# Channel mix of a two-layer graph network: each time half times one 96x96 block, in place of two 96x192 products summed in PSUM

## The chip, the core and the metric

The kernel runs on one core of a Trainium2 chip. The metric is the device time of one execution in microseconds (us); the time of a kernel is the median of its runs. Each profile shows one execution.

## What is computed

The reference is a stack of two graph convolutions, each followed by a token feed-forward part (a mixture of experts after the first, a quantised two-layer net after the second). `x` has 16 batch items, 512 nodes, 16 channels and 12 times. Each graph convolution begins with an attention over channels, whose result then multiplies the data:

```python
def _attention(x, W1, W2, requires_value):
    sh = x.shape
    xf = x.reshape(sh[0], sh[1], -1)
    dk = xf.shape[-1]
    left = xf @ W1 @ W2
    att = jnp.einsum('bnd,bmd->bnm', left, xf) / jnp.sqrt(jnp.float32(dk))
    att = jax.nn.softmax(att, axis=-1)
    return (att @ xf).reshape(sh) if requires_value else att
...
xc = jnp.swapaxes(_attention(jnp.swapaxes(x, 1, 2), W1_c, W2_c, True), 1, 2)
xt = jnp.swapaxes(_attention(jnp.swapaxes(xc, 1, 3), W1_t, W2_t, True), 1, 3)
```

The channel mix is the product `att @ xf` of the line that makes `xc`. For each batch item a 16x16 matrix mixes the channels of every node and every time; times are not mixed with each other.

## The kernel before, in words

The program is a sequence of blocks, each ended by all engines together: normalise (n0), channel attention scores (c0), channel mix (m0), time attention scores (t0), graph convolution (g0), then normalise again, routing, experts and their sum, and the second layer with c1, m1, t1, g1, and the feed-forward part at the end. The letters are the tags in the tile names (`m_ps` is the PSUM tile of m0 and m1).

`mix_channels` (L661) is the block that the change touches; it runs twice, as m0 and as m1. The normalised data of one item lie in DRAM as 192 rows (time-major: row = time x 16 + channel) by 512 nodes. They are loaded as two halves of 96 rows: `xnT[z][0:96, h, :]` has times 0 to 5 for h = 0 and times 6 to 11 for h = 1. Four such buffers rotate (`z`).

- **SyncE** (L672) issues the loads of items 0 to 3 (L677), then two loads for later stages (`late_loads`, L183: `wt`, L186, and `adj`, L187, 1 MB each), then for each following item a load (L682) when TensorE is done with the item four before it (`mixed`).
- **VectorE** (L686) makes the moving operand: `big_matrix(b)` spreads the mixing matrix of item b (`rct`, 96 rows by 16 channels) over 192 columns (channel x 12 + time), zero where row and column have different times (`tmask`), in two operations (L693), one for each half of the rows. Two buffers (`big`, shown as `L_k`) rotate, so item b waits for `mixed` of item b - 2. In m1 it also does work of the `Ternary` class between the blocks: sums of magnitudes of the last feed-forward weights (L1830, three chunks after each of the blocks 2 to 6, the last after 7), their scale (L1840 to L1847) after block 9, and the rounding (L1853 to L1860, two chunks after each block from 10 on, four more at the end).
- **TensorE** (L721) takes for item b, for each of four node groups of 128, the two halves as stationary operands (96x128) and the two blocks as moving operands (96x192), and sums the two products in PSUM (L730). A product of f32 operands shows in the trace as two weight loads and two matmuls. The PSUM tile has two buffers. In m1 a product that sums the magnitudes across partitions (`across`) stands between items 7 and 8.
- **ScalarE** (L745) copies an item's 128x768 result to `shared` (L751). The next block (t0 or t1) begins with projections from `shared` (L590).

Outside the block three other products matter for reading costs: the residual product of the graph convolution (L900), which takes the same `xnT` halves with 97 rows against 96 columns; the logits of the second normalise (L421), 96 stationary columns against 8 moving ones; and products of the identity with itself (`keep_awake`, L287). The routing's product L1253 writes its 128 columns in runs of 8 that stand 16 apart.

Of the kernel before, what the change touches and what calls it, by code (L numbers as in the profile page):

```python
# [21 lines left out]
ALU = mybir.AluOpType  # L22
# [3 lines left out]
B, N, C, T = 16, 512, 16, 12  # L26
CT = C * T
# [6 lines left out]
P = 128  # L34
NK = N // P
HALF = CT // 2
TH = T // 2
# [24 lines left out]
def ready(n):  # L62

    return n + 1 + LEAD


def free(n, depth):

    return n + 1 + LEAD - depth


def dma_ready(i):

    return (i + 2) * 16
# [108 lines left out]
def late_loads(eng, s, d, L, late):  # L183

    p = lambda n: d[f"L{L}_conv_{n}"]
    eng.dma_start(s.wt[:, :, :, :], p("wt").rearrange("(k p) (x r) -> p k x r", p=P, r=PROJ)).then_inc(late, 16)  # L186
    eng.dma_start(s.adj[:, :, :], p("A").rearrange("(k p) m -> p k m", p=P)).then_inc(late, 16)  # L187
# [473 lines left out]
def mix_channels(nc, s, tag, xn_rows, d, L, ternary=None):  # L661

    with ExitStack() as ctx:
        (xn_in, big_done, mixed, out_done, late) = s.sems(
            tag,
            "xn_in*4 big_done mixed out_done late")
        xnT, big = [s.xnT0, s.xnT1, s.raw0, s.raw1], [s.k0, s.k1]
        psm = [ctx.enter_context(nc.psum_tensor(f"{tag}_ps{q}", [P, 2, 512], F32)) for q in range(2)]
        psq = ctx.enter_context(nc.psum_tensor(f"{tag}_psq", [P, 512], F32)) if ternary else None
        with nc.Block() as block:  # L670
            @block.sync
            def _(sp):  # L672
                for z in range(4):
                    sp.sem_inc(xn_in[z], 16)

                for z in range(4):
                    sp.dma_start(xnT[z][0:HALF, :, :], xn_rows[z]).then_inc(xn_in[z], 16)  # L677
                late_loads(sp, s, d, L, late)
                with sp.Fori(1, B // 4) as i:
                    for z in range(4):  # L680
                        sp.wait_ge(mixed, free(i * 4 + z, 4))
                        sp.dma_start(xnT[z][0:HALF, :, :], xn_rows[i * 4 + z]).then_inc(xn_in[z], 16)  # L682
                sp.wait_ge(late, 32)

            @block.vector
            def _(dve):  # L686
                dve.sem_inc(big_done, LEAD)

                def big_matrix(b):
                    if b >= 2:  # L690
                        dve.wait_ge(mixed, ready(b - 2))
                    for h in range(2):
                        last = nc.vector.tensor_tensor(  # L693
                            big[b % 2][0:HALF, h, :].rearrange("p (c t) -> p c t", t=T),
                            s.rct[0:HALF, b * C:b * C + C].unsqueeze(2).to_broadcast([HALF, C, T]),
                            s.tmask[:, h, 1, :].unsqueeze(1).to_broadcast([HALF, C, T]), ALU.mult)
                    last.then_inc(big_done, 1)

                if ternary:
                    big_matrix(0)  # L700
                    big_matrix(1)
                    ternary.begin(dve)
                    for b in range(2, HB):
                        big_matrix(b)
                        for c in range(3 * b - 6, min(3 * b - 3, 16)):
                            last = ternary.magnitude(c)
                    ternary.step(last)
                    big_matrix(HB)
                    big_matrix(HB + 1)
                    ternary.scales(dve, psq)  # L710
                    for b in range(HB + 2, B):
                        big_matrix(b)
                        ternary.round(range(2 * (b - HB - 2), 2 * (b - HB - 2) + 2))
                    for c in range(12, 16, 2):
                        ternary.round(range(c, c + 2))
                else:
                    for b in range(B):
                        big_matrix(b)

            @block.tensor  # L720
            def _(pe):  # L721
                pe.sem_inc(mixed, LEAD)

                def mix(b, z, i):
                    pe.wait_ge(xn_in[z], dma_ready(i))
                    pe.wait_ge(big_done, ready(b))
                    pe.wait_ge(out_done, free(b, 2))
                    for k in range(NK):
                        for h in range(2):
                            last = nc.tensor.matmul(psm[z % 2][:, k // 2, CT * (k % 2):CT * (k % 2) + CT],  # L730
                                                    xnT[z][0:HALF, h, P * k:P * k + P], big[z % 2][0:HALF, h, :],
                                                    start=(h == 0), stop=(h == 1))
                    last.then_inc(mixed, 1)

                with pe.Fori(0, B // 8) as i:
                    for z in range(4):
                        mix(i * 4 + z, z, i)
                if ternary:
                    ternary.across(pe, psq)
                with pe.Fori(B // 8, B // 4) as i:  # L740
                    for z in range(4):
                        mix(i * 4 + z, z, i)

            @block.scalar
            def _(act):  # L745
                act.sem_inc(out_done, LEAD)
                with act.Fori(0, B // 4) as i:
                    for z in range(4):
                        b = i * 4 + z
                        act.wait_ge(mixed, ready(b))  # L750
                        nc.scalar.activation(  # L751
                            s.shared[:, bass.ds(b * (NK * CT), NK * CT)].rearrange("p (a x) -> p a x", a=2),
                            psm[z % 2][:, :, 0:2 * CT], ACT.Copy).then_inc(out_done, 1)
# [1743 lines left out]
```

## Time and profile before

| | us |
|---|---|
| median of 3 runs | 1767.14 (1765.31 to 1768.95) |
| span of the profiled execution | 1757.2 |
| TensorE matmuls busy in it | 1443.9 (82%) |
| VectorE busy | 1063.8 (61%) |
| ScalarE busy | 769.8 (44%) |
| m0, first product to start of last eviction | 80.5 to 125.0 |
| m1, first product to end of VectorE's work | 1133.4 to 1183.1 |

Times in the trace are counted from the start of the span. PE is TensorE's matmul side, PEld its weight loads, DVE VectorE, ACT ScalarE, POOL GpSimd, SP SyncE; a q behind an engine's name is its instruction queue. Matmuls are pipelined, so the duration of one is longer than the distance to the next; a run of n that follow each other is read from start to start. The granted clock of TensorE is given in shares of 2.4 GHz: 1.00 is 2.4 GHz and 0.50 is 1.2 GHz.

### The profile page before, as it was taken

Reading aid. Unit: us, or ns where it says so; the run is one execution under the profiler, and the core shown is the slowest. Engines: PE = TensorE matmul, PEld = TensorE weight load, DVE = VectorE, ACT = ScalarE, POOL = GpSimd, SP = SyncE. Lnnn points to the kernel's source line nnn. Section 1 sums busy time; section 2 is a strip of 40 time slices with the busy share of each in tenths; the row PEclk is TensorE's granted clock in tenths of the full one; section 3 lists DMA queues with packets and bytes.
Section 4 is the critical chain, followed back from the end, with each engine's and each line's share of the span. In section 5 each row is a group of like instructions: output and inputs, shape, how many; then the busy total and the mean of one; then the engine's idle time right before and its main releaser. Section 6 shows DMA issues by size and latency. Waiting matters only on the chain. (4 is left out here: it accounts for less than half of the span.)

```text
span 1757.2 us, 27360 instructions
## 1 busy us (share of the span) xinstructions
PE 1443.9 (82%) x8574; PEld 1199.9 (68%) x8574; DVE 1063.8 (61%) x2272; ACT 769.8 (44%) x1222; POOL 610.7 (35%) x910
## 2 busy tenths in 40 slices
PE   5798999995683499999999956688999997377776
PEld 5696888885683378888888846586888886244443
DVE  5314788886446554454454326372788887478885
ACT  5323555553341132333333225222555554278885
POOL 1100465656111346655555431000356556100000
PEclk9799999998785699999999975698999999599998
DMA  7441122221662136656555368741121211112321
GB/s 244 144 122 46 48 70 72 63 81 45 200 205 92 46 97 138 128 87 131 119 111 121 46 126 298 249 110 37 46 72 63 73 61 65 62 55 81 100 88 63
DMA packets 97739, 180.14 MB, mean 103 GB/s; under 512 B 15184, under 2 KB 33152, under 8 KB 97668
## 3 DMA queue, kind: packets, MB, share of 16 engines
q1 hardware_dynamic: 75396, 135.16, 24.5%
q0 software_dynamic: 16384, 31.51, 10.5%
q10 hardware_dynamic: 5888, 12.59, 2.1%
q8 instruction: 38, 0.62, 0.2%
q14 instruction: 33, 0.27, 0.0%
HBM read 113.12 MB, written 66.10 MB: 102 GB/s over the span
## 5 line engine op out<-in xcount | busy, mean ns | idle before, releaser
L904 PE MATMUL g_y<-L_z,L_pt 128*128 128x192 f32 x1024 | 197.1, 336 | 1.5 <-ACT L_pt L1119 0.5
L904 PEld LDWEIGHTS g_y<-L_z,L_pt 128*128 128x128 f32 x1024 | 166.8, 193 | 6.8 <-ACT L_pt L1119 6.8
L1064 POOL TENSOR_TENSOR L_xr<-L_xr,L_lnb 128x192 f32<-128x192 f32 x128 | 105.6, 852 | 181.5 <-DMA L_xr<-x 95.5
L1437 POOL DMA_INDIRECT sums<-x_yo,x_places x64 | 103.0, 1609 | 136.2 <-ACT x_yo L1640 126.1
L1111 ACT ACTIVATE L_e<-g_s,L_nm 128x512 f32<-128x512 f32 x128 | 88.0, 688 | 79.7 <-DVE L_nm L952 78.1
L1549 DVE TENSOR_TENSOR x_mid<-ex_g,x_sig 128x480 f32<-128x480 f32 (+1 forms) x48 | 31.3, 653 | 135.7 <-ACT x_sig L1631 125.9
L872 PE MATMUL g_z<-L_kw,L_xnT 96*128 96x192 f32 x512 | 91.8, 331 | 20.6 <-DVE L_v L982 20.4
L1071 POOL TENSOR_TENSOR L_t<-L_rstd 128x48 f32<-128x48 f32 x96 | 28.9, 301 | 222.2 <-DVE L_rstd L1006 217.2
L872 PEld LDWEIGHTS g_z<-L_kw,L_xnT 96*128 96x128 f32 x512 | 82.3, 189 | 29.9 <-DVE L_v L982 29.9
L961 DVE SCALAR_TENSOR_TENSOR L_p<-L_e,L_rl,L_adj 128x512 f32<-128x512 f32 x128 | 99.2, 775 | 4.5
L331 POOL TENSOR_TENSOR L_rs<-L_vt,s_mhalf 96x2 f32<-96x2 f32 x48 | 33.5, 697 | 190.2 <-DVE L_vt L326 190.2
L952 DVE TENSOR_REDUCE L_nm<-g_s 128x1 f32<-128x512 f32 x128 | 87.6, 684 | 19.5 <-PE g_s L881 18.6
L2002 PE MATMUL ff_d<-s_wdn,ff_q2s 128*96 128x512 bf16 x256 | 66.4, 406 | 40.0 <-ACT ff_od L2200 40.0
L1119 ACT ACTIVATE L_pt<-g_t 128x512 f32<-128x512 f32 x128 | 75.9, 593 | 46.5 <-PE g_t L889 46.3
L889 PE MATMUL g_t<-s_ident,L_p 128*128 128x128 f32 x512 | 77.8, 275 | 9.6 <-DVE L_p L961 9.6
L1081 POOL TENSOR_TENSOR L_d<-L_d,L_lng 128x192 f32<-128x192 f32 x128 | 73.2, 604 | 35.4 <-DVE L_d L1012 35.4
L889 PEld LDWEIGHTS g_t<-s_ident,L_p 128*128 128x128 f32 x512 | 63.2, 142 | 31.2 <-DVE L_p L961 25.7
L1609 ACT ACTIVATE x_xh<-ex_t 128x480 fp32r<-128x480 f32 x64 | 36.4, 570 | 106.7 <-PE ex_t L1465 92.1
L2145 POOL TENSOR_TENSOR ff_rs<-ff_vt,s_mhalf 96x2 f32<-96x2 f32 x16 | 11.0, 688 | 206.3 <-DVE ff_vt L303 206.3
L1422 POOL DMA_INDIRECT x_xin<-xn_rows,x_index x64 | 64.7, 1012 | 51.0 <-DVE x_index L1519 18.7
L1631 ACT ACTIVATE x_sig<-ex_g 128x480 f32<-128x480 f32 (+1 forms) x48 | 27.4, 571 | 123.7 <-PE ex_g L1479 86.0
L2002 PEld LDWEIGHTS ff_d<-s_wdn,ff_q2s 128*96 128x96 bf16 x256 | 32.1, 131 | 70.8 <-issue 52.1
(337 smaller groups left out, 4034.1 us busy)
## 6 DMA issues: line engine op xcount, KB each, us to landing
L_xnT<-xn_rows SPq DMA_DIRECT2D x48, 384.0 KB, 3.4
x<-L_y SPq DMA_DIRECT2D x32, 384.0 KB, 2.6
xn_rows<-L_xnT SPq DMA_DIRECT2D x54, 192.0 KB, 3.0
L_xr<-in_x SPq DMA_DIRECT2D x24, 384.0 KB, 3.5
L_xr<-x SPq DMA_DIRECT2D x24, 384.0 KB, 3.4
L_raw<-xn_rows SPq DMA_DIRECT2D x16, 384.0 KB, 3.5
ff_xa<-x SPq DMA_DIRECT2D x16, 384.0 KB, 3.8
ff_xr<-x SPq DMA_DIRECT2D x16, 384.0 KB, 3.5
```

What stands on the lines that cost most here:

```text
L872: last = nc.tensor.matmul(psz[:, k // 2, CT * (k % 2):CT * (k % 2) + CT], xnT[q][0:HALF, h, P * k:P * k + P], kw[q][0:HALF, h, NPROJ:], st ...
L889: last = nc.tensor.transpose(pst[k % 2][:, P * c:P * c + P], pr[k % 2][:, P * c:P * c + P], s.ident[:, :])
L904: last = nc.tensor.matmul(out, pt[k % 2][:, P * c:P * c + P], z[q][:, c, :], start=False, stop=(c == NK - 1))
L952: nc.vector.tensor_reduce(s.nm2[:, k % 2:k % 2 + 1], pss[k % 2][:, :], AX, ALU.max, negate=True).then_inc(nmax_done, 1)
L961: nc.vector.scalar_tensor_tensor(out=pr[k % 2][:, :], in0=e[k % 2][:, :], scalar=s.rl[:, k % 2:k % 2 + 1], in1=s.adj[:, k, :], op0=ALU.mul ...
L1064: last = nc.gpsimd.tensor_tensor(v_, v_, gain(s.lnb), ALU.add)
L1081: last = nc.gpsimd.tensor_tensor(v_, v_, gain(s.lng), ALU.mult)
L1111: nc.scalar.activation(e[k % 2][:, :], pss[k % 2][:, :], ACT.Exp, bias=s.nm2[:, k % 2:k % 2 + 1], accum_out=s.l[:, k % 2:k % 2 + 1]).then_ ...
L1119: nc.scalar.activation(pt[k % 2][:, :], pst[k % 2][:, :], ACT.Copy).then_inc(probs_turned_sb, 1)
L1422: nc.gpsimd.indirect_dma_start(xin[t % 4][:, :], None, tokens, row(index[e % 2][:, t:t + 1])).then_inc(x_in[t % 4], 16)
L1437: nc.gpsimd.indirect_dma_start(sums, row(places[e % 2][:, 1, t:t + 1]), yo[t % 4][:, :], None, compute_op=ALU.add).then_inc(sent[t % 4], 16)
L2002: last = nc.tensor.matmul(psd[0:HALF, :], q2s[:, c, HALF * h:HALF * h + HALF], wdn[:, c, :], start=(c == 0), stop=(c == UK - 1))
```

## The change

VectorE makes one block of 96 rows by 96 columns (channel x 6 + time within the half), in one operation. Both halves of an item's rows use the same block, since row and column times are counted within the half. TensorE multiplies each half of the rows by this block and writes the 96 results into the columns of that half's times: 16 runs of 6 columns, 12 apart. Each of the two products starts and ends its own sum. The number of products, their stationary operands, the loads, the eviction and all waits stay.

```diff
                 def big_matrix(b):
                     if b >= 2:
                         dve.wait_ge(mixed, ready(b - 2))
-                    for h in range(2):
-                        last = nc.vector.tensor_tensor(
-                            big[b % 2][0:HALF, h, :].rearrange("p (c t) -> p c t", t=T),
-                            s.rct[0:HALF, b * C:b * C + C].unsqueeze(2).to_broadcast([HALF, C, T]),
-                            s.tmask[:, h, 1, :].unsqueeze(1).to_broadcast([HALF, C, T]), ALU.mult)
-                    last.then_inc(big_done, 1)
+                    nc.vector.tensor_tensor(
+                        big[b % 2][0:HALF, 0, 0:HALF].rearrange("p (c t) -> p c t", t=TH),
+                        s.rct[0:HALF, b * C:b * C + C].unsqueeze(2).to_broadcast([HALF, C, TH]),
+                        s.tmask[:, 0, 1, 0:TH].unsqueeze(1).to_broadcast([HALF, C, TH]), ALU.mult).then_inc(big_done, 1)
...
                     for k in range(NK):
+                        cols = psm[z % 2][:, k // 2, CT * (k % 2):CT * (k % 2) + CT].rearrange("p (c t) -> p c t", t=T)
                         for h in range(2):
-                            last = nc.tensor.matmul(psm[z % 2][:, k // 2, CT * (k % 2):CT * (k % 2) + CT],
-                                                    xnT[z][0:HALF, h, P * k:P * k + P], big[z % 2][0:HALF, h, :],
-                                                    start=(h == 0), stop=(h == 1))
+                            last = nc.tensor.matmul(cols[:, :, TH * h:TH * h + TH],
+                                                    xnT[z][0:HALF, h, P * k:P * k + P], big[z % 2][0:HALF, 0, 0:HALF],
+                                                    start=True, stop=True)
                     last.then_inc(mixed, 1)
```

## Rows read from the trace of the kernel before

**Rows 1.** The page: busy time of TensorE, and the chain's shares by engine.
```profile
PE 1443.9 (82%) x8574; PEld 1199.9 (68%) x8574; DVE 1063.8 (61%) x2272; ACT 769.8 (44%) x1222; POOL 610.7 (35%) x910
...
PE 7%; DVE 3%; issue 2%; ACT 2%; DMA 0%; DVEq 0%; ACTq 0%; POOL 0%; SPq 0%; POOLq 0%
```

**Rows 2.** Timeline, m0: start, length, instruction, count, idle time before and its releaser.
```profile
80.50 7.95 PE L730 MATMUL m_ps<-L_k,L_xnT 96*128 96x192 f32 x32 [4.85 <-DMA L_xnT<-xn_rows]
...
86.03 2.95 SPq L682 DMA_DIRECT2D L_xnT<-xn_rows  x2
88.12 5.23 PEld L730 LDWEIGHTS m_ps<-L_k,L_raw 96*128 96x128 f32 x32
...
91.19 0.81 ACT L751 ACTIVATE L_shared<-m_ps 128x768 f32 x1 [1.78 <-PE m_ps L730]
...
93.48 5.36 PE L730 MATMUL m_ps<-L_k,L_xnT 96*128 96x192 f32 x32
...
124.98 0.81 ACT L751 ACTIVATE L_shared<-m_ps 128x768 f32 x1 [1.79 <-PE m_ps L730]
...
126.10 5.41 PE L590 MATMUL t_psp<-L_shared,L_wt 128*32 128x192 f32 x128 [1.25 <-PEq L670]
```

**Rows 3.** Windows, m0: length, busy time by engine, PEclk, DMA share, GB/s.
```profile
80.50:85.60 5.10, 5.10 (x16) 5.10 (x17) 0.00 (x0) 0.00 (x0) 0.00 (x0) 0.50 1.05 280
85.60:124.90 39.30, 39.25 (x242) 38.95 (x240) 8.72 (x28) 12.16 (x15) 0.00 (x0) 1.00 0.54 158
```

**Rows 4.** Timeline, m1 and the start of t1.
```profile
1133.42 8.83 PE L730 MATMUL m_ps<-L_k,L_xnT 96*128 96x192 f32 x32 [5.76 <-DMA L_xnT<-xn_rows]
...
1139.08 3.71 SPq L682 DMA_DIRECT2D L_xnT<-xn_rows  x2
...
1145.44 1.27 DVE L1830 TENSOR_REDUCE s_part<-L_xa 128x1 f32<-128x512 f32 x2
...
1160.72 0.62 DVE L693 TENSOR_TENSOR L_k<-L_rct,s_tmask 96x192 f32<-96x192 f32 x2 [1.36 <-PE m_ps L730]
...
1175.32 0.62 DVE L693 TENSOR_TENSOR L_k<-L_rct,s_tmask 96x192 f32<-96x192 f32 x2
1175.86 0.87 DVE L1853 TENSOR_SCALAR L_y<-L_y,s_inv 128x512 f32<-128x512 f32 x2
...
1182.67 0.42 DVE L1860 TENSOR_SCALAR s_wdn<-L_na 128x512 bf16<-128x512 f32 x1
...
1183.39 7.69 PE L590 MATMUL t_psp<-L_shared,L_wt 128*32 128x192 f32 x128 [4.51 <-PEq L670]
```

**Rows 5.** Timeline: weight loads of four other products.
```profile
137.95 1.78 PEld L287 LDWEIGHTS g_y<-s_ident 128*128 128x128 f32 x8 [1.73 <-issue]
...
161.93 0.52 PEld L900 LDWEIGHTS g_y<-L_res,L_xnT 97*128 97x128 f32 x4
...
461.35 1.46 PEld L421 LDWEIGHTS n_psl<-s_wr,L_na 128*96 128x96 f32 x16
...
547.13 1.68 PEld L1253 LDWEIGHTS rt_pre<-r_hot,r_tri 96*96 96x96 f32 x8 [7.32 <-DVE r_hot L1291]
```

**Rows 6.** DMA issues, m0, issued 79.0, 86.0, 96.4: count, KB, us to landing.
```profile
L_adj<-in_L_conv_A SPq DMA_DIRECT2D x1, 1024.0 KB, 11.9
...
L_xnT<-xn_rows SPq DMA_DIRECT2D x1, 384.0 KB, 6.4
...
L_xnT<-xn_rows SPq DMA_DIRECT2D x1, 384.0 KB, 3.2
```

**Rows 7.** Timeline, n0: VectorE's 96x96 product.
```profile
58.11 0.25 DVE L258 TENSOR_TENSOR L_res<-L_y,s_tmask 96x96 f32<-96x96 f32 x1
```

**Rows 8.** DMA issues, m1: the load issued at 1139.1.
```profile
L_xnT<-xn_rows SPq DMA_DIRECT2D x1, 384.0 KB, 7.7
```

**Rows 9.** Windows, the end of m1 and the start of t1.
```profile
1181.30:1184.70 3.40, 1.31 (x20) 0.96 (x24) 1.72 (x5) 0.00 (x0) 0.00 (x0) 0.50 0.02 5
```

**Rows 10.** Windows, the first part of n0.
```profile
13.90:31.00 17.10, 9.38 (x81) 7.54 (x79) 9.58 (x35) 12.94 (x18) 4.12 (x6) 1.00 0.89 280
```

## The prediction

> **What bounds the kernel now.** I read the page first [rows 1]. TensorE is busy for 82% of the span, but that is an average over stages with other limits, and the chain that ended last reaches back through the feed-forward tail alone (its engine shares add up to about 14%), so it says nothing of the mix. The change touches two stages, m0 of the first convolution and m1 of the second; I read each from its timeline.
>
> In m0 [rows 2] the first TensorE instruction waits for the first load and starts at 80.50. From 88.12 on the weight loads follow each other without a gap: 32 in 5.23 us, the last one 0.19 long, so (5.23 - 0.19)/31 = 0.163 us from one to the next. One batch item is 16 of them (8 products, two passes each for f32), 2.60 us. ScalarE's eviction waits 1.78 us of that for TensorE. Items 4 to 15 run from 93.48 at that pace, the last eviction starts at 124.98 and t0's first product at 126.10. So TensorE sets m0's end. Only the first item ran slowly: up to 85.6 the granted clock is 0.50, behind it 1.00 [rows 3].
>
> m1 is different [rows 4]. TensorE starts at 1133.42 and is done at 1183.39 - 4.51 = 1178.9, but t1's first product starts at 1183.39 only: VectorE's rounding of the feed-forward weights ends at 1182.67 + 0.42 = 1183.1. VectorE waits 1.36 us for TensorE before item 10's block at 1160.72; the five blocks after it come every (1175.32 - 1160.72)/5 = 2.92 us, the last without idle time before it. So m1's end is set by VectorE, which enters its last long run only when TensorE lets it.
>
> **What an item costs on TensorE afterwards.** The stationary operand (96x128) and the number of products stay; each product moves 96 columns instead of 192. The trace has nearly this shape: the residual product of L900 takes the same activations, 97x128, against 96 columns [rows 5]. Its four weight loads take 0.52 us, (0.52 - 0.19)/3 = 0.110 each. That isn't half of 0.163, and the logits product shows why: with 8 moving columns and 96 stationary ones it still takes (1.46 - 0.165)/15 = 0.086. A short product is paced by its weight load. I take 0.111 for 16 in a row; an item is 1.78 us. The Trainium skill ("TensorE: Matmul & The Clock Gate", section "LDWEIGHTS") lets a load's time go with the stationary columns, which speaks against counting on half the columns; its figure gives an estimate of 107 ns for 128 columns, 1.71 us an item, and by it m0 would gain another 0.8 us; the rows agree within 4 ns. At the lower clock 128 columns both ways come every (1.78 - 0.33)/7 = 0.207 us, the first step being short; I take 0.213, 3.41 us an item.
>
> The result is now written in 16 runs of 6 columns, 12 apart. The nearest row is L1253, which writes runs of 8, 16 apart: its eight steps take (1.68 - 0.28)/7 = 0.20 us at the lower clock, no more than the contiguous 0.207 for as many columns. Price 0; the upper bound, since no row has this at the higher clock, is today's 0.163 (each column as dear as two), which is a rival below.
>
> **m0, step by step.** Item 0: 80.5 + 3.4 = 83.9. Item 1 is half at the lower clock (it rose at 85.6): 86.5. Items 2 and 3: 90.1. Item 4 needs its own load, and here a wait appears that is hidden today. The two late loads (wt, adj, 1 MB each) are queued on SP ahead of it; adj, issued at about 79.0, needs 11.9 us and lands near 91.0 [rows 6]. Load 4 was issued at 86.03 [rows 2], five us before that, and needed 6.4 us: 92.4. DMA is fully used by then (share 1.05 in 80.5 to 85.6 [rows 3]), so asking 2 us sooner brings nothing. (The Trainium skill, "DMA: Bandwidth & Descriptors", section "Specifications", says each DMA engine consumes its ring in order; without that order load 4 could come up to 1.7 us sooner. Its landing right behind adj agrees with the rule.) Today item 4 starts at 93.48, so this load has 1.1 us of slack; then TensorE stands 92.4 - 90.1 = 2.3 us. From 92.5 on, 12 x 1.78 = 21.4: last product about 113.9, against 93.48 + 12 x 2.60 = 124.7 now. Gain 10.8. Later loads keep up: they need 3.2 us [rows 6], and from the end of item b to the start of b + 4 there are 3 x 1.78 = 5.3. The eviction (0.81 and 0.1 to 0.2 to start) and the builder (below) fit inside 1.78.
>
> **The block builder.** It was two operations of 96x192 done in 0.62 us, which keep VectorE for 1175.86 - 1175.32 = 0.54 [rows 4]; it becomes one of 96x96. The nearest row is the residual weights' product of L258, 0.25 us [rows 7]. Neighbours overlap by some 0.08 (0.62 against 0.54), so it keeps VectorE for about 0.17. Per item VectorE gets back 0.37. In m0 that is worth nothing: TensorE is the pace and VectorE waits there.
>
> **m1, step by step.** Items 0 and 1 at the lower clock end at 1140.2, items 2 and 3 at 1143.9. Load 4 was issued at 1139.08 and needed 7.7 us [rows 8], behind the same two late loads: 1146.8, so TensorE stands 2.9 us. Items 4 to 7 end at 1146.9 + 7.1 = 1154.0. VectorE's three magnitude sums an item (1.27 for two: 0.6 each [rows 4]) and the block, 2.0 us, are a little over 1.78, but the stall gives VectorE some 2.5 us of lead. The sum across partitions (0.15) and item 8 follow to 1156.0, so item 10's block starts at 1156.1 instead of 1160.72: 4.6. From there VectorE is the bound, and six blocks save 0.37 each: 2.2. Gain 6.8. TensorE ends about 1171 and VectorE at 1176.3; the rest of TensorE's saving in m1 is lost.
>
> **The two stalls and the clock.** After m1 TensorE has nothing for 4.51 us, and the stretch behind it runs at 0.50 [rows 9]; L590 takes 7.69 us there [rows 4], 5.41 in t0 at full clock [rows 2]. The new stalls of 2.3 and 2.9 us may do the same; each would put an item at 3.41 instead of 1.78, 1.6 us. I count one of them. For a clock that otherwise stays up: in 13.9 to 31 TensorE is busy 9.38 of 17.10 us, 55%, and the clock is 1.00 [rows 10], while the new items follow without gaps. t1 starts behind such an idle time now too; at worst L590 would run wholly at the lower clock (2 x 5.41, 3.1 us more than now). I take 0.
>
> **Sum.** 10.8 + 6.8 - 1.6 = 16.0 us. The profiled span would go from 1757.2 to 1741.2; the median of the runs is 9.9 above that span, and with the same around it the time is 1767.1 - 16.0 = 1751.1.
>
> **Rivals.**
> - *The weight load is not the pace* and an item takes 16 x 0.085, 1.36 us: 12 x 0.42 = 5.0 more in m0 (less what the loads then hold back, about 1), 2 more in m1, no clock lost: 23.5 together, 1743.6. The 8-column row speaks against it. 0.05.
> - *The clock falls in m1's second half*, where TensorE would work 1.78 of every 2.55 us. At 3.41 an item TensorE is the bound again from item 8: it starts at 1155.8 (one item lost to the stall), 27.3 to 1183.1, an eviction to 1184.1, 1.0 later than now. With 9.2 left in m0 8.2 in all, 1758.9. The 55% of [rows 10] speak against it, the stall ahead of it for it. 0.13.
> - *The change doesn't give what it says*: the interleaved write keeps 0.163. Then only load 4's slack and the shorter block are left, 0.9 in m0 and 2.2 in m1: 3.1, 1764.0. 0.05.
> - *Slower*: weight-paced products never bring the clock up. Today's first items do, with columns moving all the time; the new ones would move columns 0.16 of every 0.21 us there. Then m0 ends at 80.5 + 16 x 3.41 = 135.1, 10.4 later, and m1 at 1133.4 + 54.6 + 1.0 = 1189.0, 5.9 later: 16.3, 1783.4. It decides from the point where an item costs more than 2.60. Against it the same 55%. 0.05.
>
> **How the numbers follow.** The forecast has 0.72, with 13 to 20 us of gain: two, one or no item lost to the clock, and a us or two in other stages whose clock steps fall elsewhere. 1746 to 1762 holds this and the second rival and leaves 0.15 out. A measurement tells about 0.2% (3.5 us) from no change: faster 0.72 + 0.05 + 0.13 = 0.90, the third rival counts as same, 0.05, slower 0.05.
>
> **What would show it.** L730's weight loads 0.11 apart; a wait of 2 to 3 us for the load before item 4 in both stages; m0's evictions 1.8 us apart and t0 starting near 115.3; in m1 the builder every 2.55 us without idle time, and t1 starting near 1166 on the new axis (1183.4 less 10.8 and 6.8) or up to 3 later. Wrong if the loads stay 0.16 apart, if load 4 lands earlier than I say, or if the clock is 0.50 behind either stall for longer than an item.

## The result: slower, because the clock stays low in both mix stages

The changed kernel takes 1781.25 us (median of 4 runs, 1779.53 to 1789.57) where the kernel before takes 1766.22 (median of 4): a ratio of 1.0101, 95% interval 1.0053 to 1.0149. It got slower by 15.0 us; 16.0 us faster was forecast. The time lies near the rival that was called slower (1783.4), which had a chance of 0.05.

The page of the changed kernel, its busy times and the granted clock in 40 slices of the span (tenths of full speed):

```profile
PE 1465.8 (82%) x8574; PEld 1222.6 (69%) x8574; DVE 1053.1 (59%) x2240; ACT 770.5 (43%) x1222; POOL 609.6 (34%) x910
...
PEclk8657999999685589999999975657999999689999
```

The products move half the columns, and TensorE is busy 22 us longer than in [rows 1]. The slices are too coarse to say why; the two stages show it. Windows of the changed kernel over m0 and over m1, columns as in [rows 3]:

```profile
82.30:136.90 54.60, 54.55 (x256) 54.55 (x256) 3.57 (x14) 12.16 (x15) 0.00 (x0) 0.50 0.49 140
1148.00:1202.70 54.70, 53.66 (x251) 53.43 (x251) 30.17 (x80) 12.17 (x15) 0.00 (x0) 0.50 0.50 139
```

PEclk is 0.50 from end to end in both, where [rows 3] show 0.50 for the first 5 us and 1.00 for the next 39. The timeline of the changed kernel (the mix product is now on L729, the builder on L692, the eviction on L750):

```profile
82.35 7.14 PE L729 MATMUL m_ps<-L_k,L_xnT 96*128 96x96 f32 x32 [4.95 <-DMA L_xnT<-xn_rows]
...
89.13 6.95 PEld L729 LDWEIGHTS m_ps<-L_k,L_raw 96*128 96x128 f32 x32
...
93.04 0.81 ACT L750 ACTIVATE L_shared<-m_ps 128x768 f32 x1 [2.60 <-PE m_ps L729]
...
138.53 7.13 PE L590 MATMUL t_psp<-L_shared,L_wt 128*32 128x192 f32 x128 [1.25 <-PEq L670]
...
1162.71 7.14 PE L729 MATMUL m_ps<-L_k,L_xnT 96*128 96x96 f32 x32 [1.03 <-ACT L_shared L750]
...
1197.61 0.26 DVE L692 TENSOR_TENSOR L_k<-L_rct,s_tmask 96x96 f32<-96x96 f32 x1 [0.77 <-PE m_ps L729]
...
1204.54 0.81 ACT L750 ACTIVATE L_shared<-m_ps 128x768 f32 x1 [2.60 <-PE m_ps L729]
...
1205.66 7.74 PE L590 MATMUL t_psp<-L_shared,L_wt 128*32 128x192 f32 x128 [1.25 <-PEq L670]
```

Against [rows 2]: 32 weight loads take 6.95 us instead of 5.23, (6.95 - 0.33)/31 = 0.2135 each, 3.41 us an item where 2.60 was. The columns alone would take 96/192 of the 0.32 that a step took at the lower clock before; the step is the weight load's. Against [rows 4]: VectorE now waits 0.77 us for TensorE before item 15's block, and the eviction at 1204.54 is the last thing before t1; m1's bound has gone from VectorE to TensorE.

The row at 1162.71, item 4 of m1, is one to read with care. The 1.03 us are put down to ScalarE, whose eviction of item 3 (1161.81) ended just before it. But with two PSUM buffers item 4 needs the eviction of item 2 (1158.40), which had ended 3.5 us earlier. The load of item 4 was issued at 1151.60 and took 10.9 us (DMA issues of the changed kernel, columns as in [rows 6]), so it landed at 1162.5: the wait is the load's.

```profile
1158.40 0.81 ACT L750 ACTIVATE L_shared<-m_ps 128x768 f32 x1 [2.60 <-PE m_ps L729]
...
1161.81 0.81 ACT L750 ACTIVATE L_shared<-m_ps 128x768 f32 x1 [2.60 <-PE m_ps L729]
```

```profile
L_xnT<-xn_rows SPq DMA_DIRECT2D x1, 384.0 KB, 10.9
```

Where the time came from, from stage to stage. Each stage is measured from the first projection (L590) of the attention before it to that of the attention behind it, which leaves most of the rest of the program out (the projections of c0 and c1 themselves are in it, and in some of the later profiles they take 6.9 to 8.1 us instead of 5.4):

| us | c0 to t0 | c1 to t1 | both against before |
|---|---|---|---|
| before | 63.3 | 68.6 | |
| changed | 74.0 | 75.1 | +17.2 |

t0's projections follow at the lower clock, 7.13 us instead of 5.41, another 1.7. These 18.9 us are the change's share of the 20.5 by which the two profiled spans differ (1777.7 and 1757.2).

### The profile page after: what moved, and what is told of

Same layout as the page of the kernel before. It is cut to its first block and busy times, and to the rows that moved or that the text cites. A ratio compares the mean times of both kernels' runs of the same rounds, so it can differ in the third digit from the quotient of the medians.

```text
span 1777.7 us, 27328 instructions
## 1 busy us (share of the span) xinstructions
PE 1465.8 (82%) x8574; PEld 1222.6 (69%) x8574; DVE 1053.1 (59%) x2240; ACT 770.5 (43%) x1222; POOL 609.6 (34%) x910
## 5 line engine op out<-in xcount | busy, mean ns | idle before, releaser
L871 PE MATMUL g_z<-L_kw,L_xnT 96*128 96x192 f32 x512 | 91.8, 331 | 20.8 <-DVE L_v L981 20.5
L951 DVE TENSOR_REDUCE L_nm<-g_s 128x1 f32<-128x512 f32 x128 | 87.5, 683 | 21.1 <-PE g_s L880 20.3
L2001 PE MATMUL ff_d<-s_wdn,ff_q2s 128*96 128x512 bf16 x256 | 63.6, 393 | 40.0 <-ACT ff_od L2199 40.0
L888 PEld LDWEIGHTS g_t<-s_ident,L_p 128*128 128x128 f32 x512 | 63.3, 141 | 30.7 <-DVE L_p L960 25.3
L899 PEld LDWEIGHTS g_y<-L_res,L_xnT 97*128 97x128 f32 x512 | 76.1, 195 | 6.4 <-ACT L_y L1124 1.1
L1478 PE MATMUL ex_g<-x_xh,x_guh 128*128 128x480 f32 (+1 forms) x192 | 76.6, 399 | 3.1 <-issue 3.1
```

Of the source, the lines that this page charges most:

```text
L871: last = nc.tensor.matmul(psz[:, k // 2, CT * (k % 2):CT * (k % 2) + CT], xnT[q][0:HALF, h, P * k:P * k + P], kw[q][0:HALF, h, NPROJ:], st ...
L888: last = nc.tensor.transpose(pst[k % 2][:, P * c:P * c + P], pr[k % 2][:, P * c:P * c + P], s.ident[:, :])
L899: nc.tensor.matmul(out[:, HALF * h:HALF * h + HALF], xnT[q][0:HALF + 1, h, P * k:P * k + P], s.res[0:HALF + 1, h, :], start=(h == 0), stop ...
L951: nc.vector.tensor_reduce(s.nm2[:, k % 2:k % 2 + 1], pss[k % 2][:, :], AX, ALU.max, negate=True).then_inc(nmax_done, 1)
L1478: last = nc.tensor.matmul(ps_[z][0:size, 0:SN], w[:, k, off + at:off + at + size], x[q][:, k, SN * c:SN * c + SN], start=(k == 0 and x is ...
L2001: last = nc.tensor.matmul(psd[0:HALF, :], q2s[:, c, HALF * h:HALF * h + HALF], wdn[:, c, :], start=(c == 0), stop=(c == UK - 1))
```

## The experiments

Theory A: products of 96 columns, paced by their weight load, don't bring the clock up. Theory B: the interleaved write to PSUM keeps the stage slow. Theory C: the mix would hold a clock that is up. A fourth one, D, came out of the first runs. A stage is given as above; the tables at the end of this section have all of them.

### Is it the interleaved write?

Two runs take it from both sides. The first takes the runs away and leaves the 96 columns:

```diff
-                        cols = psm[z % 2][:, k // 2, CT * (k % 2):CT * (k % 2) + CT].rearrange("p (c t) -> p c t", t=T)
+                        cols = psm[z % 2][:, k // 2, CT * (k % 2):CT * (k % 2) + CT]
...
-                            last = nc.tensor.matmul(cols[:, :, TH * h:TH * h + TH],
+                            last = nc.tensor.matmul(cols[:, HALF * h:HALF * h + HALF],
```

> The changed kernel, but each half's 96 result columns are written contiguously (the order of the columns in the result is left as written, so the following stages get permuted columns). Theory A, products paced by their weight load do not bring the clock up: granted clock 0.50 through m0 and m1, weight loads 0.213 us apart, an item 3.41 us, time as the changed kernel, about 1781. Theory B, the interleaved PSUM write keeps the stage slow: the clock rises behind the first items, loads 0.11 apart, time near 1751.

Windows of m0 with contiguous writes:

```profile
81.40:135.80 54.40, 54.40 (x255) 54.40 (x256) 3.57 (x14) 12.17 (x15) 0.00 (x0) 0.50 0.49 141
```

The same kernel's timeline, the weight loads of two items:

```profile
88.14 6.95 PEld L729 LDWEIGHTS m_ps<-L_k,L_raw 96*128 96x128 f32 x32
```

0.50 throughout and the same 6.95 us for 32. c0 to t0 is 73.9 us, as with the runs (74.0). The time, 1790.64 in its one run, is above the expected 1781. The two stages don't differ; 9.8 of the 11.1 us by which the two spans differ are in the second normalise (last section).

The second keeps the 192 columns, in the order of the time halves, and writes them in runs:

```diff
...
-                            last = nc.tensor.matmul(psm[z % 2][:, k // 2, CT * (k % 2):CT * (k % 2) + CT],
+                            last = nc.tensor.matmul(psm[z % 2][:, k // 2, CT * (k % 2):CT * (k % 2) + CT].rearrange(
+                                                        "p (c g t) -> p g c t", g=2, t=TH),
```

> The kernel before, with its 192 moving columns ordered by time half and written to PSUM in runs of 6 columns, 12 apart, as the change writes; the two products are still summed. Theory A: as before, loads 0.163 apart at full clock, 1766 within 4 us. Theory B: the clock stays at 0.50 in both stages, loads 0.32 apart, an item 5.1 us, some 35 to 40 us more for each stage, near 1840.

Windows of m0 with 192 columns in runs:

```profile
83.00:88.30 5.30, 5.26 (x16) 5.26 (x17) 0.00 (x0) 0.00 (x0) 0.00 (x0) 0.50 1.04 259
88.30:127.10 38.80, 38.80 (x240) 38.80 (x240) 8.72 (x28) 12.16 (x15) 0.00 (x0) 1.00 0.56 162
```

Its timeline, the weight loads of two items:

```profile
95.96 5.23 PEld L731 LDWEIGHTS m_ps<-L_k,L_xnT 96*128 96x128 f32 x32
```

The clock rises behind the first item as it did before, 32 loads take the same 5.23 us, the stages 63.7 and 68.8. Time 1773.15 in one run, 3 us above the expected range, with 1763.71 to 1775.82 for the kernel before on that chip; the second normalise is 9.3 us longer in this profile than in that of before. Theory B has fallen: the write in runs of 6 costs nothing, with 192 columns at 1.00 (5.23 us for 32 loads in both) or with 96 at 0.50 (6.95 in both).

### Is it the number of columns beside a weight load?

The block gets 8 columns a channel, two of them zero, and the results a pitch of 14; the two halves of a channel overlap by zero columns. A product moves 128 columns, as many as its weight load has. The eviction leaves the padding out (not shown).

```diff
+TW, PITCH = 8, 14
...
-                        big[b % 2][0:HALF, 0, 0:HALF].rearrange("p (c t) -> p c t", t=TH),
+                        big[b % 2][0:HALF, 0, 0:C * TW].rearrange("p (c t) -> p c t", t=TW),
...
-                            last = nc.tensor.matmul(cols[:, :, TH * h:TH * h + TH],
-                                                    xnT[z][0:HALF, h, P * k:P * k + P], big[z % 2][0:HALF, 0, 0:HALF],
+                            last = nc.tensor.matmul(cols[:, :, TH * h:TH * h + TW],
+                                                    xnT[z][0:HALF, h, P * k:P * k + P], big[z % 2][0:HALF, 0, 0:C * TW],
...
```

> The changed kernel, but the block has 8 columns for each channel (128 columns, two of eight zero) and the results stand 14 apart in PSUM (runs of 8, overlapping by the zero columns); the eviction drops the padding. A product moves 128 columns beside a weight load of 128. Theory A: at the lower clock columns move for all of the 0.213 us a step, the clock rises as before, loads 0.111 apart, an item 1.8 us, with a wait of 2 to 3 us for load 4: 1751, between 1746 and 1758. Theory B: 0.50 throughout, 1781 as the changed kernel. Theory C as B.

1753.0 us (4 runs), ratio 0.9897, 0.9860 to 0.9933: a third more columns than in the changed kernel, and the two stages take 28 us less (121.1 against 149.1). Windows of m0 (before the clock rises, behind it, items 4 and 5, the rest):

```profile
82.70:88.20 5.50, 5.49 (x25) 5.50 (x26) 0.29 (x1) 0.81 (x1) 0.00 (x0) 0.50 1.03 281
88.20:92.50 4.30, 4.30 (x40) 4.30 (x39) 0.57 (x2) 1.62 (x2) 0.00 (x0) 1.00 1.05 376
95.00:101.90 6.90, 6.90 (x32) 6.90 (x33) 0.29 (x1) 0.81 (x1) 0.00 (x0) 0.51 0.60 159
101.90:119.60 17.70, 17.70 (x161) 17.70 (x160) 2.60 (x9) 8.10 (x10) 0.00 (x0) 1.00 0.55 156
```

Its timeline, with the wait for load 4 in m0 and, as the last row, in m1:

```profile
94.98 7.09 PE L730 MATMUL m_ps<-L_k,L_xnT 96*128 96x128 f32 x32 [2.25 <-DMA L_xnT<-xn_rows]
...
105.37 3.65 PEld L730 LDWEIGHTS m_ps<-L_k,L_xnT 96*128 96x128 f32 x32
...
1151.63 6.19 PE L730 MATMUL m_ps<-L_k,L_xnT 96*128 96x128 f32 x32 [3.75 <-DMA L_xnT<-xn_rows]
```

Three things are to be seen. At the lower clock 26 weight loads take 5.5 us, 0.21 each, the same step as with 96 columns; what differs is the columns that move in it (and the runs of the write and the reading of the eviction, which takes 0.81 us as before), and the clock rises. At the higher clock a step is (3.65 - 0.19)/31 = 0.112. And item 4 waits 2.25 us for its load; behind that wait items 4 and 5 run at 0.51, 3.5 us each. In m1 the wait is 3.75 us, and the two items behind it take 6.2 us where two at 1.00 take 3.7. Theory A holds; what remains open is whether 96 columns would hold the clock.

### Do 96 columns hold a clock that is up?

Identity products ahead of item 0, where TensorE waits some 5 us for the first load, bring it up:

```diff
+                keep_awake(nc, s, psm[1][:, 0, 2 * CT:2 * CT + P], 20)
```

> The changed kernel with 20 identity products (128x128, 40 steps) ahead of item 0 in both stages, so that TensorE is at the higher clock when the mix begins. Theory A: the clock falls back to 0.50 a few us into the mix and stays there; time 1778 to 1786. Theory C, the mix holds a clock that is up and only fails to raise it: loads 0.111 apart from the start or after load 4, time 1750 to 1758.

Windows of m0: items 0 to 3, the wait for load 4, the rest.

```profile
83.70:90.80 7.10, 7.10 (x66) 7.10 (x64) 0.77 (x3) 2.43 (x3) 0.00 (x0) 1.00 1.05 345
90.80:94.80 4.00, 0.19 (x2) 0.03 (x1) 0.25 (x1) 0.81 (x1) 0.00 (x0) 0.72 1.06 245
94.80:135.60 40.80, 40.77 (x191) 40.78 (x192) 2.55 (x10) 8.92 (x11) 0.00 (x0) 0.50 0.29 82
```

1791.41 us in one run. Four items at 1.78 us with the clock at 1.00, then 3.8 us without work, and 0.50 for all the rest. The time is above theory A's 1778 to 1786 (the second normalise is 11.1 us longer than in the changed kernel's profile), and A's reason didn't come: the clock fell at the wait, and then never rose again. So I formed theory D: these products can't raise the clock, but hold it while nothing interrupts them.

The next run takes the wait away by moving the two late loads on SP's queue, one behind the load of item 7, the other behind that of item 11 (the warm products of the run above stay, 20 of them):

```diff
...
-                late_loads(sp, s, d, L, late)
-                with sp.Fori(1, B // 4) as i:
+                for i in range(1, B // 4):
...
+                    if i < 3:
+                        late_loads(sp, s, d, L, late, i - 1)
```

> The changed kernel (96 columns) with 20 identity products ahead of item 0 and the late loads moved, so that it starts at the higher clock and has no wait before item 4. Theory C, the mix holds a clock that is up: 0.111 a step through both stages, 1740 to 1748. Theory A in its strong form, weight-paced 96-column products neither raise nor hold it: the clock falls to 0.50 some items into the stage without any wait, 1765 to 1780.

Windows of m0, items 0 to 6 and items 8 to 15:

```profile
85.10:98.00 12.90, 12.69 (x114) 12.52 (x113) 1.70 (x7) 4.94 (x7) 0.00 (x0) 1.00 0.68 204
103.50:130.60 27.10, 27.08 (x127) 27.09 (x128) 1.53 (x6) 5.67 (x7) 0.00 (x0) 0.50 0.34 102
```

The timeline at item 8:

```profile
103.52 2.81 PE L732 MATMUL m_ps<-L_k,L_xnT 96*128 96x96 f32 x12 [3.23 <-DMA L_xnT<-xn_rows]
```

The time, 1771.65 in one run, lies in the range of the strong form of theory A, but not for its reason, a fall without a wait: the wait had only moved, to item 8, whose load now queues behind `wt`. But the clock held for eight items up to that wait, and for none behind it.

With both late loads behind the last load of the mix no item waits (14 identity products, again ahead of item 0):

```diff
-                late_loads(sp, s, d, L, late)
                 with sp.Fori(1, B // 4) as i:
...
+                late_loads(sp, s, d, L, late)
...
+                keep_awake(nc, s, psm[1][:, 0, 0:0 + P], 14)
```

> The changed kernel (96 columns) with 14 identity products ahead of item 0 in both stages and the two late loads issued on SP behind the last load of the mix, so that no item waits. Theory D, such products can't raise the clock but hold one that is up while nothing interrupts them: m0 at 0.111 a step for all 16 items, from the projections of c0 to those of t0 50 to 52 us (63.3 before, 74.0 changed). In m1 VectorE interrupts them from item 10 on (1.8 us of every 2.55): the clock holds up to there; if it falls behind, an item takes 3.4 us and c1 to t1 is 64 to 68 us, if not 60 to 62. Strong form of theory A, they can't hold it either: it falls within m0 without any wait, c0 to t0 over 60.

Windows: m0, then m1 in three parts (to item 9, items 10 to 13, items 14 and 15).

```profile
84.40:112.80 28.40, 28.40 (x257) 28.40 (x256) 3.57 (x14) 12.16 (x15) 0.00 (x0) 1.00 0.79 221
1142.50:1160.60 18.10, 18.10 (x164) 18.10 (x164) 13.37 (x36) 7.29 (x9) 0.00 (x0) 1.00 0.72 192
1160.60:1169.50 8.90, 7.79 (x66) 7.31 (x65) 8.66 (x26) 3.52 (x5) 0.00 (x0) 1.00 0.82 241
1169.50:1176.30 6.80, 6.76 (x32) 6.77 (x32) 6.59 (x18) 1.34 (x2) 0.00 (x0) 0.50 0.61 222
```

The timeline of m1 and the start of t1:

```profile
1164.13 0.25 DVE L692 TENSOR_TENSOR L_k<-L_rct,s_tmask 96x96 f32<-96x96 f32 x1
...
1166.68 0.25 DVE L692 TENSOR_TENSOR L_k<-L_rct,s_tmask 96x96 f32<-96x96 f32 x1
...
1167.06 2.02 PE L729 MATMUL m_ps<-L_k,L_xnT 96*128 96x96 f32 x16 [0.53 <-DVE L_k L692]
1169.54 7.14 PE L729 MATMUL m_ps<-L_k,L_raw 96*128 96x96 f32 x32 [0.45 <-DVE L_k L692]
...
1178.76 0.42 DVE L1860 TENSOR_SCALAR s_wdn<-L_na 128x512 bf16<-128x512 f32 x1
...
1179.49 7.17 PE L590 MATMUL t_psp<-L_shared,L_wt 128*32 128x192 f32 x128 [2.81 <-PEq L670]
```

1748.48 us, ratio 0.9891, 0.9843 to 0.9939. The very products of the change, warmed and uninterrupted, do all 16 items of m0 in 28.4 us at 1.00. In m1 VectorE's blocks interrupt them from item 12 on (by 0.17, 0.53 and 0.45 us), and the clock falls for the last two items. Theory D holds in both parts. c1 to t1 is 58.2, below both numbers that I expected: the fall came so late that TensorE is done at 1176.7, while t1 begins at 1179.49, behind the end of VectorE's work at 1179.2. The fall cost nothing.

The control is the same kernel without its last added line, the identity products:

> The changed kernel with only the late loads issued last, no identity products. Theories A and D: no wait, but the clock is low at the start and is never raised: 3.41 us an item, c0 to t0 74, c1 to t1 75, as the changed kernel. If the low clock came from the load of SP's queue or of DMA, it would rise.

Windows of m0 of the control:

```profile
82.00:136.40 54.40, 54.37 (x255) 54.37 (x256) 3.57 (x14) 12.15 (x15) 0.00 (x0) 0.50 0.48 141
```

0.50 throughout, stages 73.7 and 74.9 us, 1795.18 in one run. Neither the order of the loads nor a wait keeps the clock down, nor does DMA: its share is 0.48 here, and it was 0.79 in the warmed kernel at 1.00. The clock starts low, and these products don't raise it.

### What the late loads cost, and a version that beats both

The kernel before, with nothing but its late loads moved behind the loads of items 7 and 11 (the diff on SP's queue shown above, alone):

> The kernel before with only the late loads moved. TensorE sets the pace at 2.60 us an item and load 4 has 1.1 us of slack there, so both theories say no change: 1767, within 3 us.

1764.04 us, ratio 0.9987, 0.9955 to 1.0018: no change. At 2.60 us an item the order of the loads doesn't matter.

The same move in the kernel with 128 columns:

> The 128-column version with the two late loads moved on SP's queue: wt behind the load of item 7, adj behind that of item 11, so that no load of the mix queues behind them. If the wait of about 2 us (m0) and 4 us (m1) before item 4, and the lower clock behind it, are the late loads' doing, both go: the clock stays at 1.00 once it is up, m0 ends some 6 us sooner than in the 128-column version, m1 5 to 8, time 1739 to 1745. If the loads alone can't keep 1.8 us an item, the waits move behind the late loads and 1748 to 1755 remains.

1756.69 us, ratio 0.9961, 0.9934 to 0.9989. The expectation was missed: the waits did move behind the late loads, and the time is even above the 1748 to 1755 given for that. The two stages take 3.6 us less than with 128 columns and the late loads in place (117.5 against 121.1), yet the ratio to before was lower there (0.9897). The ten runs of this version alone spread over 1751.98 to 1767.89 us, so the medians can't tell such a difference. Its timeline at item 8, of m0 and of m1:

```profile
98.90 7.09 PE L733 MATMUL m_ps<-L_k,L_xnT 96*128 96x128 f32 x32 [1.67 <-DMA L_xnT<-xn_rows]
...
1153.52 5.46 PE L733 MATMUL m_ps<-L_k,L_xnT 96*128 96x128 f32 x32 [1.43 <-DMA L_xnT<-xn_rows]
```

The window behind the wait in m0, items 8 and 9:

```profile
98.90:105.80 6.90, 6.90 (x32) 6.90 (x33) 0.29 (x1) 0.81 (x1) 0.00 (x0) 0.51 1.06 296
```

Item 8 waits 1.67 us instead of item 4's 2.25, and again two items follow at 0.51, 3.5 us each instead of 1.8. In m1 the wait is 1.43 us, and the two items behind it take 5.46 us instead of 3.7. So each of these waits costs 1.7 to 3.4 us of lower clock on top of itself.

And warmed as well:

```diff
+                keep_awake(nc, s, psm[1][:, 0, 0:0 + P], 14)
                 with pe.Fori(0, B // 8) as i:
```

> The 128-column version with moved late loads and 14 identity products ahead of item 0 in both stages, while TensorE would wait for the first load. They end up to 2 us behind that load's landing and bring the clock up, which saves 1.6 us for each of the first one or two items: 1 to 5 us less than without them, 1736 to 1743; if the first loads (1.6 us apart) are the pace there, nothing.

1756.24 us, ratio 0.9931, 0.9904 to 0.9958: this expectation was missed too. m0 gained (52.8 us against 55.4); m1 lost it (68.0 against 62.1): the identity products ended 3.3 us behind the start that m1 had without them, and the wait at item 8 was 5.55 us instead of 1.43.

Last, 128 columns with both late loads behind the last load of the mix, first without identity products, then with them in m0 alone:

```diff
-                late_loads(sp, s, d, L, late)
                 with sp.Fori(1, B // 4) as i:
...
+                late_loads(sp, s, d, L, late)
                 sp.wait_ge(late, 32)
```

> The 128-column version with the late loads issued last. No item waits, the clock rises behind the first items and stays: 1.79 us an item, c0 to t0 52 to 54 us, c1 to t1 58 to 61, in all 18 to 22 us less than before.

```diff
+                if not ternary:
+                    keep_awake(nc, s, psm[1][:, 0, 0:0 + P], 14)
                 with pe.Fori(0, B // 8) as i:
```

> As the one before it, with 14 identity products ahead of item 0 in m0 only (in m1 they ended 3.5 us behind the first load's landing). One or two items of m0 come 1.6 us sooner each, the products end 1 to 2 us late: c0 to t0 51 to 53, c1 to t1 as without them.

1746.12 us, ratio 0.9873, 0.9834 to 0.9911, and 1751.35, ratio 0.9884, 0.9832 to 0.9936. The intervals overlap with each other and with that of the 96 columns kept warm; all three beat the kernel before by 1.1 to 1.3% in the ratio, while the change alone lost 1.0%. The stages came as expected without identity products (53.7 and 59.0); those in m0 gained 0.3 us, less than expected. The window of m0 behind the rise of the clock, in the one without identity products:

```profile
86.70:112.10 25.40, 25.40 (x230) 25.40 (x229) 3.76 (x13) 11.34 (x14) 0.00 (x0) 1.00 0.78 224
```

Its timeline, the end of m0 and two blocks of m1:

```profile
112.61 0.81 ACT L751 ACTIVATE L_shared<-m_ps 128x768 f32 x1 [0.98 <-PE m_ps L730]
...
116.77 3.75 PE L590 MATMUL t_psp<-L_shared,L_wt 128*32 128x192 f32 x44 [4.30 <-PEq L670]
...
1163.36 0.28 DVE L692 TENSOR_TENSOR L_k<-L_rct,s_tmask 96x128 f32<-96x128 f32 x1
...
1163.78 2.05 PE L730 MATMUL m_ps<-L_k,L_xnT 96*128 96x128 f32 x16 [0.53 <-DVE L_k L692]
...
1165.95 0.28 DVE L692 TENSOR_TENSOR L_k<-L_rct,s_tmask 96x128 f32<-96x128 f32 x1
```

The clock stays up once it has risen, and no item waits for its load. Now the late loads are late themselves: the last eviction ends at 113.4, t0 begins at 116.77 and its projections take 7.39 us instead of 5.41 [rows 2], which the table doesn't count. In m1 VectorE is the bound, 2.59 us from block to block; it interrupts TensorE by up to 0.53 us, as with 96 columns, but here the clock stays at 1.00. A version that splits the two late loads so that `adj` is waited for only in the graph convolution wasn't tried.

| us | c0 to t0 | c1 to t1 | both against before |
|---|---|---|---|
| 96 columns, contiguous | 73.9 | 75.0 | +17.0 |
| 192 columns in runs | 63.7 | 68.8 | +0.6 |
| 96 columns, warmed | 74.9 | 76.0 | +19.0 |
| 96, warmed, late loads behind items 7 and 11 | 69.4 | 69.2 | +6.7 |
| 96, warmed, late loads last | 52.6 | 58.2 | -21.1 |
| 96, late loads last | 73.7 | 74.9 | +16.7 |
| 128 columns | 56.0 | 65.1 | -10.9 |
| 128, late loads behind items 7 and 11 | 55.4 | 62.1 | -14.4 |
| 128, the same, warmed | 52.8 | 68.0 | -11.1 |
| 128, late loads last | 53.7 | 59.0 | -19.2 |
| 128, late loads last, m0 warmed | 53.4 | 58.6 | -19.9 |
| before, late loads behind items 7 and 11 | 63.6 | 68.5 | +0.2 |

## Why the prediction was wrong

- **The bounds of the two stages** were read rightly: TensorE in m0, VectorE behind TensorE in m1. Both show again in the versions that keep the clock.
- **The item at the higher clock**, 0.111 a step and 1.78 us, was right (0.112 measured with 96 and with 128 columns), and so was the reason, the weight load. The estimate from the Trainium skill ("TensorE: Matmul & The Clock Gate", section "LDWEIGHTS"), 0.107, would have been 4% low. At the lower clock 0.213 was right too (0.2135).
- **The write in runs at no price** was right, at both clocks.
- **The block** costs 0.26 us (0.25 forecast), and VectorE's period in m1 is 2.55 us in the warmed kernel with 96 columns (1166.68 - 1164.13), as forecast. With 128 columns it is 2.59.
- **The wait for load 4** was right as a mechanism and near in size where items are fast: 2.25 us in m0 with 128 columns (2.3 forecast), 3.75 in m1 (2.9 forecast). Load 4 of that m0 was issued at 86.67 and needed 8.1 us behind the late loads; with the late loads last, such loads need 3.3 us (first and second line below). The order of a ring, which the prediction takes from the Trainium skill, "DMA: Bandwidth & Descriptors", stands there in the section "Queues, rings and completion order", not in "Specifications". The 1.7 us given beside it are shown by no run. In the changed kernel's m0 the wait doesn't occur, as the items are slower than the loads; in its m1 it is 1.03 us.

```profile
L_xnT<-xn_rows SPq DMA_DIRECT2D x1, 384.0 KB, 8.1
...
L_xnT<-xn_rows SPq DMA_DIRECT2D x2, 384.0 KB, 3.3
```

- **The step that failed is the one on the clock.** The sums for m0 and m1 take over the rise of the clock from the trace of before ("it rose at 85.6") and let every item behind it run at 1.78 us. In the changed kernel the clock doesn't rise, and all 32 items take 3.41. I set the paragraph "for a clock that otherwise stays up" on [rows 10], where TensorE is busy for 55% of a stretch at 1.00. That stretch shows other products under a clock that was already up; it says nothing of what raises a low one. The changed stage is busy for 54.55 of 54.60 us and has 0.50, so the busy share didn't answer the question: it counts a step that waits for its weights like one that moves columns. What did bear on it was in the prediction, in the rival's line: 0.16 of 0.21 us with columns moving, against all of it before. I gave this 0.05 where nothing in the trace of before showed such products raising the clock. The rival's price was right: 16.3 forecast, 17.2 in the stages, 15.0 in the medians. It left out t0's projections (1.7).
- **The price of a wait** was too small: one item at 3.41 for each (1.6 us), one of the two counted. With 128 columns the two items behind a wait take 1.7 to 3.4 us more than at 1.00; with 96 all that are left run at the lower clock. The 128-column version, whose clock does rise, therefore gains 7.4 us in m0 and 3.5 in m1, 10.9 together, and not 16.0: even where the clock rises, as the prediction took for granted, the sum for the two stages was too high, as far as a kernel with 128 columns can show it.
- **The rival of the second half of m1** (VectorE interrupts, the clock falls) is real, but late and small: two items in the warmed version with 96 columns, at no cost, none with 128.

## What to carry to other kernels

Halving the columns of a product that is paced by its weight load buys less than half even at best (0.163 to 0.112 us a step here), and at the lower clock it can end the rise of the clock that the longer product brought about. So look at what the engine did just before the clock rose, not at a busy share under a clock that is already up; and if a short product is wanted, let it move as many columns as its weight load has (128 did it here), or warm TensorE in a wait ahead of it. Then look for the loads queued ahead of the one that faster items need: each wait costs its length and the items at the lower clock behind it.

## What was not expected of the hardware

- Raising and holding differ. 96-column steps hold 1.00 for 28.4 us without a break and don't leave 0.50 in 54 us; 128-column steps of the same 0.213 us leave it after 5.5 us. Counts between 96 and 128 weren't tried. In m1 interruptions of 0.45 and 0.53 us were followed by 0.50 with 96 columns; with 128 columns the same interruptions left the clock at 1.00.
- A wait of 1.67 us was followed by 6.9 us at 0.51.
- The second normalise, which no kernel here touches, differs from profile to profile: from its first logits product to its last it takes 78.1 us in the profile of before, 77.7 in the changed one, 87.5 with contiguous writes, 87.4 with 192 columns in runs, 88.8 and 89.9 in the first warmed kernel and in the control, and 95.1 in that with 128 columns, the late loads last and m0 warmed. With one profile for each kernel it isn't shown whether the kernel or the execution makes this difference; 24 of the 25 runs of the kernel before on one chip spread over 1758.31 to 1778.72 us. That is why stages are compared here. Single runs of kernels with the changed kernel's stages came out at 1790.64 and 1795.18.
